# Two mixtures of experts in one pipeline: the second mixture's routing is started one group earlier and spread out

## The chip, the cores and the metric

One core of one Trainium2 chip runs the whole program. The metric is the device time of one execution in microseconds (us). Engines: PE is TensorE (matmul), PEld its weight load, DVE is VectorE, ACT is ScalarE, POOL is GpSimd, SP is SyncE, which only starts DMAs here.

## The reference

The program computes an attention layer, a chunked delta-rule layer and two mixtures of experts, each on x of 8 batches x 512 tokens x 256 channels. The change is in the last part, the two mixtures in a row:

```python
# mixture 0 (cond2): 8 experts of 128, 2 chosen, 256 shared hidden units
logits = (x @ wt.T + g @ wg.T) / 2
scores = softmax(logits); topk_w, topk_idx = top_k(scores, 2); topk_w /= topk_w.sum()
y = sum_k topk_w * (leaky(x @ w_gate[e]) * (x @ w_up[e])) @ w_down[e]   + shared
# mixture 1 (ffn): 16 experts of 64 in 4 groups, 2 groups and then 4 experts chosen, 512 shared units
scores = sigmoid(y @ router_w.T); sb = scores + correction_bias
group_scores = top_k(sb in 4 groups, 2).sum(-1); keep the 2 best groups
topk_idx = top_k(masked sb, 4); w = scores[topk_idx] / sum
out = x + sum_e combine[e] * (silu(y @ gate_w[e]) * (y @ up_w[e])) @ down_w[e]   + shared
```

## The kernel before

`mixtures_phase` works batch by batch. A **group** (m, b) is mixture m on the 512 tokens of batch b. The 16 groups run in the order (0,0), (0,1), (1,0), (0,2), (1,1), ..., (0,7), (1,6), (1,7), so a pair (0,b+1), (1,b) is the steady pattern. A group is cut into **items**, 128 hidden units each: 10 for mixture 0 (items 0 and 1 shared, 8 of one expert each), 12 for mixture 1 (items 0 to 3 shared, 8 of two experts each); 176 items in all. `FIRST[g]` is the first item of group g; q counts items over all groups.

Every engine walks the same list of q, each with an instruction queue of its own, and semaphores order them:

- PE at q: 6 matmuls for the gate (`m_G`) and 6 for up (`m_U`), both L1380 (fp32 as high and low parts), then the side steps of q, then `project_down(q - 2)`, 6 matmuls of the item two back (`m_Y`, L1397). `project_down` waits for `hid_high` and `hid_low` of its item.
- ACT at q: the activation of the gate (L1446; Copy for mixture 0, Silu for mixture 1), its side steps, then the high part of item q-1 (`high`, L1434), then DMA starts of the routing weights (L1480 writes `wT` to DRAM, L1491 reads them back, spread over partitions).
- DVE at q: for mixture 0 the leaky ReLU (L1603), then times up (L1605), for routed items times the routing weights (`weigh`, L1584), its side steps, and at the end the **routing parts** of q (`PARTS[q]`, function `route`).
- POOL at q: the low part of the item (L1523), after ACT's high part.

Side steps (`SIDE[q]`) share one PSUM bank `MB` in the order of the list, each waiting until the one before has been read (`m_bank_free`): `turn` (transpose of x for a batch to come, L1312), `logits` (6 router matmuls, L1329), `rows` (4 small transposes of the logits, L1338, and the exponential on ACT), `weights` (4 transposes of the routing weights, L1347, copied by DVE at L1629 to `wT`), `back` (transposes of the result, L1358, added to x by DVE at L1636). `W_AT[g]` is the item whose side step is `weights` of group g.

The routing parts of mixture 0 are three (`spread`, `choose`, `weigh`), those of mixture 1 are seven: `scores` (ends in a ranking within groups), `groups`, then four rankings `choose0` to `choose3`, one for each 128 tokens (`rank_below`, L997 to L1002, six DVE instructions), and `weigh` (L1572 to L1576). In the kernel before, the logits of (1,b) are computed in item 2 of the mixture 0 group right ahead of it, and the seven parts follow in seven items in a row, 4 to 9 of that group and item 0 of (1,b). The weights of (1,b) are turned at its item 2, the first routed item being item 4. Where a group ends, ACT and DVE take its result out of PSUM in item 1 of the next (`taken_at`).

Of the kernel before, what the change touches and what calls it, by code (L numbers as in the profile page):

```python
# [92 lines left out]
def row(ap, n):  # L93

    return bass.AP(tensor=ap.tensor, offset=ap.offset, ap=[[0, P], [1, n]])
# [909 lines left out]
def mixtures_phase(nc, a, ident, mixture, shared_sems, x1_dram, w_dram, out):  # L1005

    F32R = mybir.dt.float32r
    with ExitStack() as ctx:
# [121 lines left out]
        w_ready = sem("w_ready")  # L1130
# [22 lines left out]
        NG = len(GROUPS)  # L1153
# [8 lines left out]
        SIDE, PARTS, W_AT = {}, {}, {}  # L1162

        def side(q, *steps):
            SIDE.setdefault(q, []).extend(steps)

        def route_from(g, q):

            m = GROUPS[g][0]
            for n, part in enumerate(("spread", "choose", "weigh") if m == 0 else  # L1170
                                     ("scores", "groups", "choose0", "choose1", "choose2", "choose3", "weigh")):
                PARTS.setdefault(q + n, []).append((part, g))
# [5 lines left out]
        PARTS[-1] = [(part, 0) for part in ("spread", "choose", "weigh")]  # L1178
        for g, (m, b) in enumerate(GROUPS):
            q0 = FIRST[g]  # L1180
            W_AT[g] = q0 + (0 if g < 2 else -1 if m == 0 else 2)
            side(W_AT[g], ("weights", g))
            if g == 0:
                side(q0 + N1 - 1, ("turn", 1, 0), ("turn", 1, 1))
                side(q0 + N1 - 1, ("logits", 1), ("rows", 1))
                PARTS[q0 + N1 - 1] = [(part, 1) for part in ("spread", "choose", "weigh")]
            elif m == 0:
                at = 3 if b == 1 else 2
                side(q0 + at, ("logits", g + 1))
                side(q0 + at + 1, ("rows", g + 1))  # L1190
                route_from(g + 1, q0 + at + 2)
                if b >= 2:
                    side(q0 + 4, ("back", b - 2, 0))
                    side(q0 + 5, ("back", b - 2, 1))
            elif b < B - 2:
                side(q0 + 2, ("turn", b + 2, 0))
                side(q0 + 3, ("turn", b + 2, 1))
                side(q0 + 5, ("logits", g + 1))
                side(q0 + 6, ("rows", g + 1))
                route_from(g + 1, q0 + 7)  # L1200
            elif b == B - 2:
                side(q0 + 4, ("logits", g + 1))
                side(q0 + 5, ("rows", g + 1))
                route_from(g + 1, q0 + 6)
            else:
                side(q0 + 4, ("back", b - 1, 0))
                side(q0 + 5, ("back", b - 1, 1))
# [7 lines left out]
        def nth(step):  # L1215

            same = [s for s in FILLS if s[0] == step[0]]
            return same.index(step) + 1
# [5 lines left out]
        def n_shifted(g):  # L1224

            return sum(GROUPS[s[1]][0] == 0 for s in FILLS[:FILLS.index(("rows", g)) + 1] if s[0] == "rows")
# [20 lines left out]
        def routed(q):  # L1247
            g, m, b, i = ITEMS[q]
            return i >= SHARED[m]

        def n_routed(q):

            return sum(routed(j) for j in range(q + 1))
# [19 lines left out]
        with nc.Block() as block:  # L1273
# [149 lines left out]
            @block.scalar  # L1423
            def _(act):
                def high(q):

                    if routed(q):
                        act.wait_ge(weighted, n_routed(q))
                    else:
                        act.wait_ge(mult_up, q + 1)  # L1430
                    if q >= H_SLOTS:

                        act.wait_ge(hid_used, q - H_SLOTS + 1)
                    act.copy(hid_part[0][:, q % H_SLOTS], hid[:, q % G_SLOTS]).then_inc(hid_high, 1)  # L1434

                late = [(lower[:], a["c_lower"]), (cb[:], row(a["L0_ffn_correction_bias"], E2))]
                assert len(late) == N_LATE
                for dst, src in late:
                    act.dma_start(dst, src).then_inc(loaded_late, 16)
                for q in QS:  # L1440
                    if 0 <= q < NQ:
                        act.wait_ge(gate_psum, q + 1)
                        if q >= G_SLOTS:

                            act.wait_ge(hid_low, q - G_SLOTS + 1)
                        act.activation(hid[:, q % G_SLOTS], GB[q % 2][:, :],  # L1446
                                       (ACT.Copy, ACT.Silu)[ITEMS[q][1]]).then_inc(gate_active, 1)
                    for step in SIDE.get(q, ()):
                        if step[0] == "split":
                            m, part, s, (high_w, _, given_w), _, _ = units[step[1]]  # L1450
                            act.wait_ge(w_in[m][part][s], 16 * sum(u[:3] == (m, part, s) for u in units))
                            act.copy(high_w, given_w).then_inc(w_high, 1)
                        elif step[0] == "turn":
                            act.wait_ge(turned, nth(step))
                            act.copy(in0[0][:, step[2]], MB[:, :]).then_inc(in0_high, 1)
                        elif step[0] == "logits":
                            m, b = GROUPS[step[1]]
                            act.wait_ge(logits_psum, nth(step))
                            if m == 0:
                                act.activation(lgT[0:E1, :], MB[0:E1, :], ACT.Identity, scale=0.5,  # L1460
                                               bias=condg[:, b:b + 1]).then_inc(lgT_ready, 1)
                            else:
                                act.copy(lgT[:, :], MB[0:E2, :]).then_inc(lgT_ready, 1)
                        elif step[0] == "rows":
                            m, b = GROUPS[step[1]]
                            if m == 0:
                                act.wait_ge(shifted, n_shifted(step[1]))
                                act.activation(ex[:, :, 0:E1], lg[:], ACT.Exp).then_inc(exps_ready, 1)
                            else:
                                act.wait_ge(rows_psum, nth(step))  # L1470
                                act.activation(ex[:], MB[:, 0:TT * E2].rearrange("p (t e) -> p t e", e=E2), ACT.Exp,
                                               scale=-1.0).then_inc(exps_ready, 1)
                    if 0 <= q - 1 < NQ:
                        high(q - 1)
                    for step in SIDE.get(q, ()):
                        if step[0] == "weights":
                            g = step[1]
                            n = NE[GROUPS[g][0]]
                            act.wait_ge(wT_ready, nth(step))
                            act.dma_start(w_dram[g % 2, 0:n], wT[g % 2][0:n]).then_inc(wT_out, 16)  # L1480
                    for at in W_LOADS.get(q, ()):
                        g, m, b, item = ITEMS[at]
                        slot = (n_routed(at) - 1) % W_SLOTS
                        act.wait_ge(wT_out, 16 * nth(("weights", g)))
                        if n_routed(at) > W_SLOTS:

                            act.wait_ge(weighted, n_routed(at) - W_SLOTS)
                        for e in range(1 + m):
                            part = slice(e * M2, e * M2 + M2) if m else slice(0, P)
                            one = w_dram[g % 2, (1 + m) * (item - SHARED[m]) + e, :]  # L1490
                            act.dma_start(spread[part, slot], bass.AP(tensor=one.tensor, offset=one.offset,  # L1491
                                                                      ap=[[0, part.stop - part.start], [1, L]]))\
                               .then_inc(spread_in[slot], 16)
                    g = taken_at(q)
                    if g is not None:

                        m, b = GROUPS[g]
                        act.wait_ge(hid_used, FIRST[g + 1])
                        if m == 0:
                            for k in range(KD):  # L1500
                                act.copy(in1[b % 2][0][:, k], YB[k][:, :]).then_inc(y_act, 1)
                        else:
                            if b > 0:
                                act.wait_ge(rows_back, 2 * b)
                            act.copy(outT[:, 0], YB[0][:, :]).then_inc(y_act, 1)
# [1084 lines left out]
```

## Time and profile before

| | us |
|---|---|
| median of 3 runs | 2650.97 |
| lowest, highest | 2647.69, 2654.67 |
| the profiled execution | 2649.22 |
| its span in the trace | 2647.4 |
| part of it in the mixtures (first matmul at 1773.1) | 874.3 |
| PE idle in the mixtures waiting for POOL's low part | 24.2, in 25 waits |
| PE idle there waiting for `wT` | 10.2, in 6 waits |

The durations below are those of the profiled execution. Where PE works without a gap, an item shows its first gate matmul 4.2 us after that of the item before it, so the distance between first gate matmuls tells what each item cost.

### The profile page before, as it was taken

How to read it: one execution, taken by the hardware profiler on the slowest of the kernel's cores; microseconds unless marked ns; L12 is line 12 of the kernel's file. 1: busy time of each engine (PE TensorE's matmuls, PEld its weight loads, DVE VectorE, ACT ScalarE, POOL GpSimd, SP SyncE). 2: the span in 40 equal slices, each digit the busy share in tenths (PEclk: the TensorE clock that was granted, in tenths of full speed). 3: DMA queues.
4: the chain of work that ended last, by engine and by line, in shares of the span. 5: the costliest groups of instructions: out<-in, count | busy, mean ns of one | idle time of the engine just before them, and what ended most of it. 6: DMA issues, size and time to landing. Idle time of an engine off the chain costs nothing. (4 is left out here: it accounts for less than half of the span.)

```text
span 2647.4 us, 56555 instructions
## 1 busy us (share of the span) xinstructions
PE 2431.2 (92%) x20838; PEld 2014.3 (76%) x20838; DVE 1711.6 (65%) x4060; ACT 1217.7 (46%) x3095; POOL 1338.6 (51%) x1465
## 2 busy tenths in 40 slices
PE   5999999999999999759999999978899999999998
PEld 3788888888888888537777778856677777777776
DVE  4577677767676767567666766336756747657574
ACT  2666666666666666444544444123333233333332
POOL 3677676767676768166555555215422222322222
PEclk8999999999999999869999999979999999999999
DMA  4000100000000000001122111225021112111211
GB/s 139 7 10 9 44 17 10 10 10 10 10 13 9 7 5 6 13 13 38 46 54 54 41 40 44 64 81 143 23 72 57 49 57 61 61 49 52 64 39 57
DMA packets 156687, 105.03 MB, mean 40 GB/s; under 512 B 85168, under 2 KB 134832, under 8 KB 156416
## 3 DMA queue, kind: packets, MB, share of 16 engines
q1 hardware_dynamic: 131072, 62.83, 8.8%
q10 hardware_dynamic: 25344, 38.60, 4.9%
q8 instruction: 169, 2.77, 0.4%
q14 instruction: 102, 0.84, 0.1%
HBM read 80.51 MB, written 20.88 MB: 38 GB/s over the span
## 5 line engine op out<-in xcount | busy, mean ns | idle before, releaser
L1523 POOL TENSOR_TENSOR m_hid_part<-m_hid,m_hid_part 128x512 fp32r<-128x512 f32 x176 | 239.6, 1361 | 589.6 <-ACT m_hid_part L1434 589.5
L920 POOL TENSOR_TENSOR a_bm<-a_bias,a_mask_add 128x512 f32<-128x512 f32 (+3 forms) x512 | 438.3, 873 | 190.7 <-DVE a_nm L674 186.3
L830 ACT ACTIVATE a_S<-a_S,a_nm 128x512 f32<-128x512 f32 (+3 forms) x512 | 289.3, 565 | 346.7 <-DVE a_nm L674 343.8
L674 DVE CUSTOM_DVE_ANT_0 a_S<-a_S,a_bm,a_nsn 128x512 f32<-128x512 f32 (+3 forms) x512 | 275.6, 545 | 141.5 <-PE a_S L438 137.3
L461 PE MATMUL a_O<-a_v,a_PT 128*128 128x64 f32 x2560 | 342.3, 265 | 0.0
L461 PEld LDWEIGHTS a_O<-a_v,a_PT 128*128 128x128 f32 x2560 | 328.3, 193 | 0.1
L438 PE MATMUL a_S<-a_kT,a_qT 128*128 128x384 f32 (+3 forms) x1024 | 284.2, 359 | 3.5 <-DVE a_nm L674 3.0
L1397 PE MATMUL m_Y<-m_hid_part,m_down_high 128*128 128x512 f32 x704 | 258.6, 408 | 24.9 <-POOL m_hid_part L1523 24.2
L1446 ACT ACTIVATE m_hid<-m_G 128x512 f32<-128x512 f32 x176 | 105.3, 598 | 349.5 <-PE m_G L1380 325.1
L1380 PE MATMUL m_G<-m_in,m_gate_high 128*128 128x512 f32 x704 | 253.0, 400 | 2.5 <-POOL m_up_low L1517 1.6
L1380 PE MATMUL m_U<-m_in,m_up_high 128*128 128x512 f32 x704 | 250.5, 396 | 1.7 <-DVE m_hid L1605 1.7
L448 PE MATMUL a_T<-s_ident,a_S 128*128 128x128 f32 x1280 | 227.0, 275 | 12.3 <-ACT a_PT L839 11.3
L1605 DVE TENSOR_TENSOR m_hid<-m_hid,m_U 128x512 f32<-128x512 f32 x176 | 120.9, 687 | 176.1 <-PE m_U L1380 130.1
L448 PEld LDWEIGHTS a_T<-s_ident,a_S 128*128 128x128 f32 x1280 | 160.3, 140 | 42.3 <-ACT a_S L830 15.7
L1397 PEld LDWEIGHTS m_Y<-m_hid_part,m_down_high 128*128 128x128 f32 x704 | 133.5, 190 | 66.2 <-issue 33.8
L438 PEld LDWEIGHTS a_S<-a_kT,a_qT 128*128 128x128 f32 x1024 | 164.0, 192 | 18.7 <-DVE a_nm L674 6.5
L1434 ACT CAST m_hid_part<-m_hid 128x512 fp32r<-128x512 f32 x176 | 108.4, 616 | 124.6 <-DVE m_hid L1584 103.2
L1380 PEld LDWEIGHTS m_G<-m_in,m_gate_high 128*128 128x128 f32 x704 | 134.0, 190 | 36.0 <-POOL m_up_low L1517 2.1
L1380 PEld LDWEIGHTS m_U<-m_in,m_up_high 128*128 128x128 f32 x704 | 132.6, 188 | 34.8 <-DVE m_hid L1605 2.8
L839 ACT COPY a_PT<-a_T 128x128 f32<-128x128 f32 (+3 forms) x384 | 156.3, 407 | 0.0
L2410 DVE SCALAR_TENSOR_TENSOR d_S<-d_S,d_gm,d_state 128x64 f32<-128x64 f32 x224 | 52.4, 275 | 141.1 <-PE d_state L2139 141.0
L1380 PE MATMUL m_G<-m_in,m_gate_low 128*128 128x512 f32 x352 | 140.7, 400 | 0.0
(314 smaller groups left out, 5392.8 us busy)
## 6 DMA issues: line engine op xcount, KB each, us to landing
m_spread<-s_w ACTq DMA_DIRECT2D x64, 256.0 KB, 3.2
m_spread<-s_w ACTq DMA_DIRECT2D x128, 128.0 KB, 3.0
a_x<-in_x SPq DMA_DIRECT2D x32, 128.0 KB, 2.1
s_hT<-a_hT SPq DMA_DIRECT2D x32, 128.0 KB, 2.1
d_x<-in_x SPq DMA_DIRECT2D x8, 512.0 KB, 4.7
d_h<-s_hT SPq DMA_DIRECT2D x8, 512.0 KB, 4.0
s_xg<-d_xg SPq DMA_DIRECT2D x8, 512.0 KB, 3.0
d_x<-s_xg SPq DMA_DIRECT2D x8, 512.0 KB, 4.6
```

The costliest lines, as they stand in the source:

```text
L438: last = pe.matmul(o_s[:, 0:w], qT[:, tile % 2, h], kT[tile // TT % 2][i][:, 0:w], start=i == 0, stop=i == 1)
L448: last = pe.transpose(TB[n % 2][:, j * P:(j + 1) * P], S[:, n % S_SLOTS, j * P:(j + 1) * P], ident[:])
L461: last = pe.matmul(OB[h // 8][:, (h % 8) * DH:(h % 8 + 1) * DH], PT[:, n % PT_SLOTS, j * P:(j + 1) * P], v[tile // TT % 2][:, j], start=j ...
L674: dve.tensor_tensor_reduce(S[:, n % S_SLOTS, 0:w], SB[n % 2][:, 0:w], bm[:, n % BM_SLOTS, 0:w], -1.0, nsn[:, tile % 2, h:h + 1], ALU.add, ...
L830: act.activation(S[:, n % S_SLOTS, 0:w], S[:, n % S_SLOTS, 0:w], ACT.Exp, scale=-1.0, bias=nm[:, tile % 2, h:h + 1], accum_out=den[:, tile ...
L839: act.copy(PT[:, n % PT_SLOTS, 0:w], TB[n % 2][:, 0:w]).then_inc(s["probsT_act"], 1)
L920: pool.tensor_tensor(bm[:, n % BM_SLOTS, 0:w], bias[:, h, L - w:L], mask_add[b % 2][:, 0:w], ALU.add).then_inc(s["bm_ready"], 1)
L1380: last = pe.matmul(dst[q % 2][:, :], wts[m][j][:, k, item], x[i][:, k], start=(i, j, k) == TERMS[0], stop=(i, j, k) == TERMS[-1])
L1397: last = pe.matmul(YB[k][:, :], down[m][j][:, item, k * P:(k + 1) * P], hid_part[i][:, q % H_SLOTS], start=item == 0 and i + j == 0, stop= ...
L1434: act.copy(hid_part[0][:, q % H_SLOTS], hid[:, q % G_SLOTS]).then_inc(hid_high, 1)
L1523: pool.tensor_tensor(hid_part[1][:, q % H_SLOTS], hid[:, q % G_SLOTS], hid_part[0][:, q % H_SLOTS].bitcast(F32), ALU.subtract).then_inc(hi ...
L1605: dve.tensor_tensor(h, h, UB[q % 2][:, :], ALU.mult).then_inc(mult_up, 1)
```

## The change

Only the order of steps changes; no instruction is added or removed, apart from one wait. For mixture 1 groups (1,0) to (1,5) the list now holds, besides the steps for the mixture 0 group that follows (each moved one item earlier), those of the mixture 1 group after that: its logits in item 8, its rows in item 9, `scores` and `groups` in items 10 and 11, and `choose0` to `choose3` in items 1, 3, 5 and 7 of the mixture 0 group between them, `weigh` in item 8. The weights of groups (1,1) to (1,6) are turned in the last item of the preceding group instead of their own item 2; (1,0) and (1,7) keep item 2. `rows` makes ACT wait until the weights of the group before have been computed, since `ex` and `sc` are single buffers.

```diff
--- before.py
+++ after.py
@@ -1178,26 +1178,30 @@
         PARTS[-1] = [(part, 0) for part in ("spread", "choose", "weigh")]
         for g, (m, b) in enumerate(GROUPS):
             q0 = FIRST[g]
-            W_AT[g] = q0 + (0 if g < 2 else -1 if m == 0 else 2)
+            W_AT[g] = q0 + (0 if g < 2 else 2 if g in (2, NG - 1) else -1)
             side(W_AT[g], ("weights", g))
             if g == 0:
                 side(q0 + N1 - 1, ("turn", 1, 0), ("turn", 1, 1))
                 side(q0 + N1 - 1, ("logits", 1), ("rows", 1))
                 PARTS[q0 + N1 - 1] = [(part, 1) for part in ("spread", "choose", "weigh")]
+            elif m == 0 and b == 1:
+                side(q0 + 3, ("logits", g + 1))
+                side(q0 + 4, ("rows", g + 1))
+                route_from(g + 1, q0 + 5)
             elif m == 0:
-                at = 3 if b == 1 else 2
-                side(q0 + at, ("logits", g + 1))
-                side(q0 + at + 1, ("rows", g + 1))
-                route_from(g + 1, q0 + at + 2)
-                if b >= 2:
-                    side(q0 + 4, ("back", b - 2, 0))
-                    side(q0 + 5, ("back", b - 2, 1))
+                side(q0 + 4, ("back", b - 2, 0))
+                side(q0 + 5, ("back", b - 2, 1))
             elif b < B - 2:
                 side(q0 + 2, ("turn", b + 2, 0))
                 side(q0 + 3, ("turn", b + 2, 1))
-                side(q0 + 5, ("logits", g + 1))
-                side(q0 + 6, ("rows", g + 1))
-                route_from(g + 1, q0 + 7)
+                side(q0 + 4, ("logits", g + 1))
+                side(q0 + 5, ("rows", g + 1))
+                route_from(g + 1, q0 + 6)
+                side(q0 + 8, ("logits", g + 2))
+                side(q0 + 9, ("rows", g + 2))
+                for n, part in ((10, "scores"), (11, "groups"), (13, "choose0"), (15, "choose1"), (17, "choose2"),
+                                (19, "choose3"), (20, "weigh")):
+                    PARTS.setdefault(q0 + n, []).append((part, g + 2))
             elif b == B - 2:
                 side(q0 + 4, ("logits", g + 1))
                 side(q0 + 5, ("rows", g + 1))
@@ -1463,6 +1467,8 @@
                                 act.copy(lgT[:, :], MB[0:E2, :]).then_inc(lgT_ready, 1)
                         elif step[0] == "rows":
                             m, b = GROUPS[step[1]]
+                            if step[1] > 0:
+                                act.wait_ge(w_ready, step[1])
                             if m == 0:
                                 act.wait_ge(shifted, n_shifted(step[1]))
                                 act.activation(ex[:, :, 0:E1], lg[:], ACT.Exp).then_inc(exps_ready, 1)
```

## Rows read from the trace of the kernel before

**Rows 1.** The page's busy time of each engine, its share of the span, instructions.

```profile
PE 2431.2 (92%) x20838; PEld 2014.3 (76%) x20838; DVE 1711.6 (65%) x4060; ACT 1217.7 (46%) x3095; POOL 1338.6 (51%) x1465
```

**Rows 2.** Idle time of PE by what ended it, 1990 to 2560 us (total, times, longest).

```profile
PE m_Y L1397 <- POOL m_hid_part L1523: 16.7, 18, 1.0
PE m_M L1312 <- DVE m_wT L1629: 9.3, 5, 1.9
PE m_Y L1397 <- DVE m_in L1644: 0.7, 1, 0.7
```

**Rows 3.** PE in order of time (start us, us, line, operation); first gate matmul of items.

```profile
2207.81 0.40 PE L1380 MATMUL m_G<-m_in,m_gate_high 128*128 128x512 f32 x1
...
2213.16 0.39 PE L1380 MATMUL m_G<-m_in,m_gate_high 128*128 128x512 f32 x1
...
2218.54 0.40 PE L1380 MATMUL m_G<-m_in,m_gate_high 128*128 128x512 f32 x1
...
2223.93 0.40 PE L1380 MATMUL m_G<-m_in,m_gate_high 128*128 128x512 f32 x1
...
2229.21 0.63 PE L1312 MATMUL m_M<-s_ident,m_x_turn 128*128 128x128 f32 x4 [1.87 <-DVE m_wT L1629]
...
2231.07 0.40 PE L1380 MATMUL m_G<-m_in,m_gate_high 128*128 128x512 f32 x1
...
2235.71 0.40 PE L1380 MATMUL m_G<-m_in,m_gate_high 128*128 128x512 f32 x1
...
2254.48 0.40 PE L1380 MATMUL m_G<-m_in,m_gate_high 128*128 128x512 f32 x1
...
2267.10 0.40 PE L1380 MATMUL m_G<-m_in,m_gate_high 128*128 128x512 f32 x1
...
2271.73 0.39 PE L1380 MATMUL m_G<-m_in,m_gate_high 128*128 128x512 f32 x1
```

**Rows 4.** Busy time of each engine in two equal stretches: PE, PEld, DVE, ACT, POOL, clock.

```profile
2095.00:2200.00 105.00, 100.34 (x437) 79.20 (x436) 65.32 (x118) 34.27 (x57) 29.44 (x22) 0.98 0.18 53
2200.00:2305.00 105.00, 100.33 (x444) 79.29 (x443) 66.75 (x124) 34.40 (x57) 29.44 (x22) 1.00 0.19 57
```

**Rows 5.** DVE in order of time, items 4 to 8 of group (0,4).

```profile
2191.05 0.18 DVE L1554 TENSOR_SCALAR m_ex<-m_ex 128x64 f32<-128x64 f32 x1
...
2196.34 0.69 DVE L1605 TENSOR_TENSOR m_hid<-m_hid,m_U 128x512 f32<-128x512 f32 x1
...
2198.27 0.21 DVE L1559 TENSOR_TENSOR m_rest<-m_sbias,m_sel 128x64 f32<-128x64 f32 x1
...
2202.46 0.69 DVE L1605 TENSOR_TENSOR m_hid<-m_hid,m_U 128x512 f32<-128x512 f32 x1
...
2207.88 0.69 DVE L1605 TENSOR_TENSOR m_hid<-m_hid,m_U 128x512 f32<-128x512 f32 x1
...
2210.45 1.38 DVE L1000 TENSOR_TENSOR m_gt<-m_gt,m_ge 128x256 f32<-128x256 f32 x1
```

**Rows 6.** POOL in order of time, around the last row of rows 5.

```profile
2210.02 1.53 POOL L1523 TENSOR_TENSOR m_hid_part<-m_hid,m_hid_part 128x512 fp32r<-128x512 f32 x1 [3.86 <-ACT m_hid_part L1434]
```

**Rows 7.** DVE in order of time, a ranking of group (0,5) computed during group (1,3).

```profile
2257.58 0.69 DVE L1605 TENSOR_TENSOR m_hid<-m_hid,m_U 128x512 f32<-128x512 f32 x1 [1.02 <-PE m_U L1380]
...
2259.04 0.41 DVE L997 TENSOR_TENSOR m_gt<-m_sc 128x256 f32<-128x256 f32 x1
...
2261.19 0.18 DVE L1002 TENSOR_SCALAR m_sel<-m_sel 128x32 f32<-128x32 f32 x1
```

**Rows 8.** DVE in order of time, routing weights of group (1,3).

```profile
2223.89 0.22 DVE L1572 TENSOR_TENSOR m_w<-m_sc,m_sel 128x64 f32<-128x64 f32 x1
...
2224.81 1.27 DVE L1576 TENSOR_TENSOR m_w<-m_w,m_wsum 128x64 f32<-128x64 f32 x1
```

**Rows 9.** PE in order of time, items 2 and 4 of group (1,2).

```profile
2117.81 0.40 PE L1380 MATMUL m_G<-m_in,m_gate_high 128*128 128x512 f32 x1
...
2131.13 0.40 PE L1380 MATMUL m_G<-m_in,m_gate_high 128*128 128x512 f32 x1
```

## The prediction

> **What bounds the kernel now.** I read the page's busy times first: PE is busy 92% of the span [rows 1], so a change of order can win only what PE stands still. Next the waits of PE in the mixtures, from 1990 to 2560 us, the part that the change reorders: 18 waits for POOL's low part (16.7 us), 5 for `wT` (9.3 us) and one for DVE's subtraction of `m_in` (0.7 us) [rows 2], and nothing else. Then PE in order of time, for where these waits are [rows 3]. An item without side steps takes (2267.10 - 2254.48) / 3 = 4.21 us. In the group (1,3) and the item before it, the distances are 5.35 (item 9 of (0,4)), 5.38 (item 0), 5.39 (item 1), 7.14 (item 2), 4.64 (item 3, one `turn`). So there are three slow items, and a fourth in which `weights` and `turn` meet in the one bank: PE stands 1.87 us until DVE has copied `wT`.
>
> Last, why POOL is late. DVE's times, beside its due time, tell it. A multiplication by up is due 3.1 us after the item's first gate matmul (2254.48 to 2257.58, [rows 3, 7]). Item 7 of (0,4) started two undisturbed items before 2207.81, at 2199.4, so it was due at 2202.5; DVE did it at 2207.88 [rows 5], 5.4 late. Item 6 was due at 2198.3 and done at 2202.46, 4.2 late, and cost PE nothing; the lag of 5.4 cost 1.14 in item 9. So PE bears a lag of about 4.3 us, its two items of distance less the high and low parts. Once there, each further item with a ranking costs as much as DVE needs for it: 5.42 us from 2202.46 to 2207.88, against 4.21. DVE is the bound for some 30 us of each pair of groups, and PE for the rest: in 105 us DVE is busy only 66.8 [rows 4]. It has room, but not where its work is bunched.
>
> **The change, part by part.**
>
> Moved rankings. Taken away from DVE in six consecutive mixture 0 items and one more: `scores` with the next leaky ReLU 5.3 us (2191.05 to 2196.34), so `scores` 4.6; `groups` with it 4.2 (2198.27 to 2202.46), so 3.5; each `choose` 5.42 less multiplication and weighting (1.46, rows 7's first two) and leaky ReLU (0.7), so 3.3 [rows 5, 7]. The sum is unchanged, the place is new. In the old place `choose` is stretched: its L1000 took 1.38 us while POOL's low part ran from 2210.02 to 2211.55 [rows 5, 6]. A ranking of the same 256 elements per partition that met no POOL work took 2.35 from first start to last end (2259.04 to 2261.37) [rows 7].
>
> Is the new place too full? I carry the lag of DVE on from item 10 of (1,b), where it comes in on time:
> - item 10: 1.5 + `scores` 4.6 = 6.1 against 4.2; lag 1.9.
> - item 11: 1.5 + copy of `wT`, 0.6, + `groups` 3.5, + leaky ReLU 0.7 = 6.3 against 4.6 (one `weights`); lag 3.6 at item 0 of mixture 0.
> - item 0, shared: 1.4 against 4.2; lag 0.8.
> - item 1: multiplication, copy of the result, `choose0` at its dear price, leaky ReLU: 0.7 + 0.7 + 3.3 + 0.7 = 5.4; lag 2.0.
> - item 2: 2.2; back on time. Items 3, 5, 7 with a `choose`: 4.6 to 5.5, or 5.2 to 6.1 in item 5 with its `back`, against 4.2 and 4.6; lags of 0.4 to 1.5, each gone in the next item.
> The largest, 3.6, stays under the 4.3 that PE bears, and falls on an item without weighting, which helps the low part. So I price the new rankings at nothing; PE's matmuls cover them. With the margin of 0.7 gone, each microsecond over would cost PE one in each of the 6 pairs, 6 us in all.
>
> Whether a `choose` costs 2.35 or 3.3 there: the Trainium skill ("SBUF — State Buffer", the section "SBUF: two separate sides") has VectorE and GpSimd hold a shared port pair exclusively, so an instruction with two SBUF inputs waits for the whole of POOL's. That agrees with L1000 ending just after POOL's end. By the rule an early `choose` in a routed item is over before POOL begins and costs 2.35; by the dear row it costs 3.3. The saving is the same by both, since either lag is under 4.3.
>
> Gain of it: item 9 of six groups (0,2) to (0,7), 6 x 1.14 = 6.8 us; items 0 and 1 of (1,1) to (1,6), 6 x (1.17 + 1.18) = 14.1 us [rows 3].
>
> Moved weights. The transposes cost 4.63 - 4.21 = 0.42 (2267.10 to 2271.73, an item with `weights`), `turn` 0.43 (4.64 - 4.21). Item 2 loses 7.14 - 4.21 - 0.42 - 0.43 = 2.08 us; the 0.42 is paid in item 9 instead, where no step of the bank follows until the `turn` two items later. Five groups: 10.4 us [rows 2, 3]. In (1,6), which has no `turn`, the wait of 0.7 for `m_in` goes [rows 2]. Now `w` has to be there a whole item earlier: `weigh` runs in item 8, on PE's side due 4.2 us after item 8's due time. Lag 0.4 to 1.3, multiplication and weighting 1.5, five small instructions 1.1 (2223.89 to 2224.81, and 0.2 for the last undisturbed) or 2.2 with the last one held to 1.27 [rows 7, 8]: 3.0 to 5.0. I take 3.0 to 3.9, nothing lost; at the far end 0.8 in each of 6 groups, 5 us. Behind that wait on PE stand `project_down` and the next item.
>
> DMAs. The write of `wT` and the reads for items 4 to 6 of mixture 1 no longer start together in item 3 but one item's worth at a time from item 1, on ACT's queue. ACT's activation was not the bound there before; no gain, no loss. SP's and POOL's queues are passed by nothing.
>
> Steps moved from mixture 0 item 2 and 3 to mixture 1 items 8 and 9 (`logits`, `rows`) cost PE the same there. The exponential now comes an item after mixture 0's; Exp and Silu alternate as often. The new wait of ACT for `w_ready` stands in `rows`: ahead of it nothing is open, because `weigh` of the group ahead (item 8) ends some 3 us after its item's due time and PE's `rows` comes 4.2 after. Behind it on ACT is the high part of item 8 and the activation of item 10. Cost nothing; if `weigh` were a microsecond later than PE's transposes, those two are late by it, which the 4.3 still bears.
>
> TensorE's clock. After the 1.87 us stand in (1,2) items 2 and 3 took 13.32 us (2117.81 to 2131.13) against 11.78 in (1,3) (2223.93 to 2235.71): 1.5 us more, and the stretch around it shows a mean granted clock of 0.98 of full speed against 1.00 [rows 3, 4, 9]; of the two levels, 1.2 and 2.4 GHz, some matmuls had the lower. Without the stand I count 1.5 gained. The Trainium skill ("TensorE: Matmul & The Clock Gate", the section on HAM oscillation) asks for longer idle gaps than this before the clock falls; by it the sum would be 1.5 less, 32.0. The trace disagrees, as the fall follows the gap directly.
>
> **Sum.** 6.8 + 14.1 + 10.4 + 0.7 + 1.5 = 33.5 us. The profiled execution took 2649.22, its span 2647.4, so it becomes 2615.7. It lies 1.75 below the median of the runs, 2650.97, from which 33.5 gives 2617.5. I predict 2617.
>
> **The rivals.**
> - Stalls shrink but stay: the burst of items 10 and 11 exceeds 4.3. For: the margin is only 0.7, and the weighting is held by POOL at times. Against: the lag peaks on one item. Price 0.5 to 2 us in each of 6 groups: 2620 to 2630. Chance 0.11.
> - `w` comes late, as worked out, and the whole of item 9's gain goes as well: 5 + 6.8 to both: 2629 to 2640. Chance 0.04.
> - Nothing moves: DVE is the bound over the whole pair, so that waits only change place. Then 2651. Against: DVE 66.8 of 105 us. Chance 0.02.
> - Slower: ACT's wait for `w_ready` in item 9. If `weigh` of the group ahead came late, the activation of item 10 and so `gate_psum`'s release would hold PE. PE loses only what exceeds the tolerance; `weigh` has 1.2 us in hand, PE's tolerance is 4.3, and to pass 2659 the six pairs must lose 33.5 + 8.5 = 42 us, 7 each: so it decides only where `weigh` is 12.5 us later than the rows let it be, and then gives 2660. Chance 0.02.
> - The forecast, all stalls gone: 2617, own range 2611 to 2622. Chance 0.81.
>
> **How the numbers follow.** The range 2610 to 2630 takes in the forecast and the first rival; the runs' own spread, 3.3 below the median and 3.7 above, is within it. What a measurement of this kernel can tell from no change is about 0.3%, 8 us. Faster by more: 0.81 + 0.11 + 0.04 less a little, 0.95. Within: 0.03, the case in which nothing moves and the edge of the one above it. Slower: 0.02.
>
> **What would show it.** In the profile after: PE's waits for POOL's low part down from 25 to about 7 (those of the start and the end), the waits for `wT` down from 6 to 1; distances of 4.2 in items 0 and 1 and 4.64 in items 2 and 3 of mixture 1, 4.63 in item 9 of mixture 0; L1000 shorter in the mean; a pair of groups in 99.0 us instead of 104.6 (2117.81 to 2223.93 less the clock's 1.5, [rows 3, 9]), as 1.14 + 1.17 + 1.18 + 2.08 go. Wrong would be: waits of PE for POOL two items after items 10 and 11, at the `weights` step for `w` (L1576), or a DVE lag that does not clear in the items without a ranking.

## The result

The changed kernel took 2625.39 us (median of 4 runs, 2622.33 to 2627.34) against 2649.94 for the kernel before in the same comparison: ratio 0.9904, 95% interval 0.9887 to 0.9921, so 24.6 us faster. Forecast were 2617 (range 2610 to 2630) and a gain of 33.5 us. The profiled execution took 2626.46, span 2624.7.

Forecast and measured time differ by 8 us, and the time misses the forecast's own range of 2611 to 2622. The page's busy line after it, as [rows 1] before:

```profile
PE 2429.4 (93%) x20838; PEld 2017.6 (77%) x20838; DVE 1695.6 (65%) x4060; ACT 1215.2 (46%) x3095; POOL 1337.0 (51%) x1465
```

PE's work is what it was; only standing time went. DVE's busy time fell by 16.0 us (1711.6 to 1695.6) with the same 4060 instructions. PE's waits from 1773 to 2625 us, the whole of the mixtures (before: 24.2 us in 25 waits for POOL and 10.2 in 6 for `wT`), by what ended them; total, times, longest. The wait in the steady part alone (1964 to 2560) follows:

```profile
PE m_Y L1401 <- POOL m_hid_part L1529: 11.1, 12, 1.4
PE m_M L1351 <- DVE m_w L1582: 7.4, 3, 3.4
...
PE m_M L1316 <- DVE m_wT L1635: 0.9, 1, 0.9
```

```profile
PE m_Y L1401 <- POOL m_hid_part L1529: 3.6, 5, 0.7
```

The 18 waits for POOL and 5 for `wT` of [rows 2] are gone, but 5 new ones of 0.72 us stand in their place, and a sixth in (1,0). PE in order of time shows where, for the group (1,3), first gate matmuls of items 0, 2, 4, 6 and 7 (as [rows 3]):

```profile
2207.59 0.39 PE L1384 MATMUL m_G<-m_in,m_gate_high 128*128 128x512 f32 x1
...
2215.99 0.40 PE L1384 MATMUL m_G<-m_in,m_gate_high 128*128 128x512 f32 x1
...
2225.27 0.40 PE L1384 MATMUL m_G<-m_in,m_gate_high 128*128 128x512 f32 x1
...
2235.61 0.40 PE L1384 MATMUL m_G<-m_in,m_gate_high 128*128 128x512 f32 x1
...
2239.31 0.47 PE L1401 MATMUL m_Y<-m_hid_part,m_down_high 128*128 128x512 f32 x1 [0.72 <-POOL m_hid_part L1529]
...
2240.77 0.40 PE L1384 MATMUL m_G<-m_in,m_gate_high 128*128 128x512 f32 x1
```

Items 0 and 1 are 4.20 us each, items 2 and 3, with a `turn` each, 4.64, items 4 and 5 with logits and rows 10.34 in sum. Item 6 has no side step and takes 5.16: PE stands 0.72 us ahead of the down projection of item 4, for POOL.

The clean measure of the change is the stretch from the first gate matmul of (0,2) to that of (1,6): 1956.46 to 2526.88 before, 570.42 us, and 1964.34 to 2507.42 after, 543.08. A second profile of the changed kernel gave 543.06. The part ahead of the mixtures, which no edit here touches, ended anywhere from 1774.9 to 1790.6 in twelve profiled executions (first gate matmul of the mixtures), and from there to (0,2) it was 173.6 to 179.2 us more. So the total of one execution hides effects of a few microseconds, and the stretch doesn't.

**Why item 6.** ACT in order of time, item 5 of (1,3) after the change:

```profile
2232.48 0.60 ACT L1450 ACTIVATE m_hid<-m_G 128x512 f32<-128x512 f32 x1 [1.61 <-PE m_G L1384]
2235.77 1.28 ACT L1474 ACT_TABLE_LOAD   x1 [2.69 <-DVE m_lg L1630]
...
2237.06 0.23 ACT L1474 ACTIVATE m_ex<-m_lg 128x32 f32<-128x32 f32 x1
2237.20 0.60 ACT L1438 CAST m_hid_part<-m_hid 128x512 fp32r<-128x512 f32 x1
```

and the same step in the kernel before (its item 6):

```profile
2247.76 1.28 ACT L1468 ACT_TABLE_LOAD   x1
2250.38 0.23 ACT L1468 ACTIVATE m_ex<-m_lg 128x32 f32<-128x32 f32 x1 [1.34 <-DVE m_lg L1624]
2250.52 0.60 ACT L1434 CAST m_hid_part<-m_hid 128x512 fp32r<-128x512 f32 x1
```

### The profile page after: what moved, and what is told of

Same layout as the page of the kernel before. It is cut to its first block and busy times, and to the rows that moved or that the text cites. A ratio compares the mean times of both kernels' runs of the same rounds, so it can differ in the third digit from the quotient of the medians.

```text
span 2624.7 us, 56570 instructions
## 1 busy us (share of the span) xinstructions
PE 2429.4 (93%) x20838; PEld 2017.6 (77%) x20838; DVE 1695.6 (65%) x4060; ACT 1215.2 (46%) x3095; POOL 1337.0 (51%) x1465
## 5 line engine op out<-in xcount | busy, mean ns | idle before, releaser
L1401 PE MATMUL m_Y<-m_hid_part,m_down_low 128*128 128x512 f32 x352 | 139.8, 397 | 0.0
```

The source lines that it names most:

```text
L1401: last = pe.matmul(YB[k][:, :], down[m][j][:, item, k * P:(k + 1) * P], hid_part[i][:, q % H_SLOTS], start=item == 0 and i + j == 0, stop= ...
```

## The experiments

The ratios are to the kernel before, each with its own runs of it on the same chip. Its median there was 2652.58 us for e1 to e4, 2656.32 for e5 to e8 and 2647.67 for e9 and e10, so medians of different comparisons can't be set side by side to a few microseconds; "the stretch" is that from (0,2) to (1,6), of the profiled execution.

**e1: the two waits in the other order** (the edit shortened).

```diff
-if step[1] > 0: act.wait_ge(w_ready, step[1])
 if m == 0:
     act.wait_ge(shifted, n_shifted(step[1]))
+    if step[1] > 0: act.wait_ge(w_ready, step[1])
     ...
 else:
     act.wait_ge(rows_psum, nth(step))
+    act.wait_ge(w_ready, step[1])
```

> The changed kernel with the two waits ahead of each exponential in the other order (first for its input, then for the routing weights); nothing else. Theory: the activation table load takes over the first-named of two waits when there are two, so in the changed kernel it stands behind its input (2.7 us idle before it in item 5 of mixture 1), ends 1.28 us later and makes the high and low parts of item 4 late, 0.95 us in item 6 of each of six groups. Swapped, the load stands behind the wait that has long been met: items 6 back to 4.2 us, no wait of PE for POOL there, 5 to 6 us off the changed kernel's 2625, so about 2619.5. Rival: the 0.95 us comes from logits and rows having moved one item ahead, next to the first routed items and their DMAs; then nothing changes, 2625.

Measured: 2613.13 us (2610.19 to 2619.23), ratio 0.9852 (0.9826 to 0.9879). ACT in item 5 of (1,3), then PE's first gate matmuls of items 6 and 7:

```profile
2225.34 1.28 ACT L1474 ACT_TABLE_LOAD   x1
2227.97 0.23 ACT L1474 ACTIVATE m_ex<-m_lg 128x32 f32<-128x32 f32 x1 [1.35 <-DVE m_lg L1631]
```

```profile
2227.86 0.40 PE L1384 MATMUL m_G<-m_in,m_gate_high 128*128 128x512 f32 x1
...
2232.07 0.40 PE L1384 MATMUL m_G<-m_in,m_gate_high 128*128 128x512 f32 x1
```

(The expectation calls the wait that the load takes over the first-named; in the program it is the one written last, here that for `w_ready`, long met.) The load is back ahead of the input's wait, item 6 takes 4.21, and PE doesn't stand at all in the steady part. The stretch is 538.32 us, 4.8 less than the changed kernel's, five times 0.95. The theory holds; the median lies 12 us under the first of the changed kernel, more than item 6 can give (see e9 and e10).

**e2: the kernel before with only the new wait.**

```diff
 elif step[0] == "rows":
     m, b = GROUPS[step[1]]
+    if step[1] > 0:
+        act.wait_ge(w_ready, step[1])
```

> The kernel before with only the changed kernel's wait for the routing weights ahead of each exponential; order of steps as before. Theory of the table load: the exponential for mixture 0, computed in item 6 of mixture 1 groups, has its load 1.28 us later, of which the trace of before has some 0.6 us in hand, so item 7 grows by about 0.7 to 0.9 us in six or seven groups: 4 to 6 us slower than before, about 2655. Rival, the moved steps are to blame: no change, 2650.

Measured: 2657.66 us (2647.9 to 2667.78), ratio 1.0018 (0.9999 to 1.0037). ACT, and PE where it stands:

```profile
2247.24 1.28 ACT L1470 ACT_TABLE_LOAD   x1 [2.69 <-DVE m_lg L1626]
```

```profile
2250.77 0.47 PE L1397 MATMUL m_Y<-m_hid_part,m_down_high 128*128 128x512 f32 x1 [0.72 <-POOL m_hid_part L1525]
```

The order of steps is that of before, and the same late load and the same 0.72 us appear, in item 7 (5.17 instead of 4.21). The interval of the ratio reaches 1, but the slow item is there in all of the groups (1,0) to (1,5). So the wait alone brings it, without the moved logits and rows. The stretch is 573.73, 3.3 more than before. Five slow items are 4.8; the 1.5 of the clock's fall, which this execution had no part of, makes the difference.

**e6: the wait ahead of mixture 1's exponential alone.** DVE computes the routing weights of the group ahead earlier than mixture 0's `m_lg`, in its own order, so the one wait implies the other.

```diff
-if step[1] > 0:
+if m == 1:
     act.wait_ge(w_ready, step[1])
```

> The changed kernel with its new wait only ahead of mixture 1's exponential; ahead of mixture 0's it is left out, where the wait for its input already implies it (DVE computes both in order). Theory of the table load: mixture 0's load goes ahead of the wait again, item 6 is back to 4.2 us, the same time as with the swapped waits, 2613 to 2619, though mixture 1's load still stands behind its input: that one is covered. Rival: both loads have to be freed; then about half of the gain, 2620.

Measured: 2624.46 us (2621.03 to 2625.4), ratio 0.9876 (0.9838 to 0.9914). ACT:

```profile
2234.17 1.28 ACT L1474 ACT_TABLE_LOAD   x1
2236.80 0.23 ACT L1474 ACTIVATE m_ex<-m_lg 128x32 f32<-128x32 f32 x1 [1.35 <-DVE m_lg L1630]
```

The load is free again and the stretch is 538.33, that of e1. The median is nearly that of the first comparison of the changed kernel and misses the forecast of 2613 to 2619. The profiled execution took 9.2 us more than e1's, and 8.8 of that lie ahead of the stretch: the first gate matmul of (0,2) came at 1967.3 against 1958.5. By the items the theory holds; by the total nothing can be told.

**e3: the routing weights of mixture 1 turned in its item 2 again.**

```diff
-W_AT[g] = q0 + (0 if g < 2 else 2 if g in (2, NG - 1) else -1)
+W_AT[g] = q0 + (0 if g < 2 else 2 if m == 1 else -1)
```

> The changed kernel, but the routing weights of mixture 1 turned in its own item 2, as before; the early and spread rankings stay. It measures what of the gain is the moved weights alone. If the wait of turn for the copy of the weights is the bank's own round trip it stays at about 0.9 us in each of five groups: 4 to 5 us slower than the changed kernel, 2630. If the 1.87 us of before were all due to the bunched bank steps and not to the late DVE, they stay whole: 9 to 10 us slower, 2635. If the early rankings alone had removed it: no change, 2625.

Measured: 2630.01 us (2619.54 to 2640.74), ratio 0.9919 (0.9889 to 0.9948). PE in item 2 of (1,3), between its own and the next first gate matmul:

```profile
2208.03 0.40 PE L1384 MATMUL m_G<-m_in,m_gate_high 128*128 128x512 f32 x1
...
2212.53 0.63 PE L1316 MATMUL m_M<-s_ident,m_x_turn 128*128 128x128 f32 x4 [1.09 <-DVE m_wT L1635]
...
2214.39 0.40 PE L1384 MATMUL m_G<-m_in,m_gate_high 128*128 128x512 f32 x1
```

Item 2 takes 6.36, that is 1.30 more than its matmuls and transposes (4.21 + 0.43 + 0.42). The stretch is 549.20, 6.1 more than the changed kernel's. So of the 2.08 us of before, 1.30 is the bank's own round trip from one step to the next (transposes, DVE's copy, the next transpose) and 0.78 was the late DVE: its copy began 0.27 us after the end of the transposes here (2211.44 to 2211.71) and 1.05 before (2227.34 to 2228.39). The expected 0.9 was too little.

**e4: begun as early, but the seven parts in a row.**

```diff
-for n, part in ((10, "scores"), (11, "groups"), (13, "choose0"), (15, "choose1"), (17, "choose2"),
-                (19, "choose3"), (20, "weigh")):
-    PARTS.setdefault(q0 + n, []).append((part, g + 2))
+route_from(g + 2, q0 + 10)
```

> The changed kernel, begun as early, but the seven routing parts in seven items in a row (items 10, 11 of mixture 1 and items 0 to 4 of mixture 0) instead of the four rankings in every second item. Theory: the lag of DVE is carried from item to item; it is near 4 us after item 12, passes the 4.3 us that PE bears in items 13 to 15 and costs about 1.1 us in each of two or three items of six pairs: 14 to 20 us slower than the changed kernel, 2640 to 2645. Rival: an early start alone is enough, as nothing waits for the weights; no change, 2625.

Measured: 2671.51 us (2668.13 to 2676.53), ratio 1.0071 (1.0045 to 1.0097): slower than before, and over twice what I expected it to lose. PE in (0,4), items 2 and 5, and DVE just ahead of both waits:

```profile
2192.46 0.40 PE L1382 MATMUL m_G<-m_in,m_gate_high 128*128 128x512 f32 x1
...
2196.94 0.47 PE L1399 MATMUL m_Y<-m_hid_part,m_down_high 128*128 128x512 f32 x1 [1.51 <-ACT m_hid_part L1436]
...
2198.41 0.40 PE L1382 MATMUL m_G<-m_in,m_gate_high 128*128 128x512 f32 x1
...
2207.26 0.40 PE L1382 MATMUL m_G<-m_in,m_gate_high 128*128 128x512 f32 x1
...
2213.86 1.08 PE L1360 MATMUL m_M<-s_ident,m_outT 128*128 128x128 f32 x4 [3.62 <-DVE m_res L1640]
...
2217.30 0.63 PE L1382 MATMUL m_G<-m_in,m_gate_high 128*128 128x512 f32 x1
```

```profile
2195.50 0.69 DVE L1609 TENSOR_TENSOR m_hid<-m_hid,m_U 128x512 f32<-128x512 f32 x1
...
2196.11 0.68 DVE L1654 COPY m_outT<-m_Y 128x512 f32<-128x512 f32 x1
...
2211.70 0.69 DVE L1609 TENSOR_TENSOR m_hid<-m_hid,m_U 128x512 f32<-128x512 f32 x1
...
2213.03 0.68 DVE L1640 TENSOR_TENSOR m_res<-m_M,m_res 128x512 f32<-128x512 f32 x1
```

Item 2 is 5.95 us. The profile puts its wait of 1.51 down to ACT's high part, but this is the projection of item 0, whose low part was done at 2193.79. As the first of its group it waits also until the result of the group before is out of PSUM, and DVE's copy of that (L1654) ended at 2196.79. Item 5 is 10.0: PE stands 3.62 us ahead of the second `back`, until DVE has read the first one out of the bank (L1640 at 2213.03), and the matmuls after it take 0.63 us instead of 0.40, at a granted clock of 0.50 from 2213.9 to 2219.2, the lower of the two levels, 1.2 GHz.

Neither is a wait for the low part, which the theory looked for. It had reckoned only with the down projection of an item two back, which bears a lag of 4.3 us. DVE's multiplication of item 1 came 4.2 late (2195.50, due at 2191.3) and cost 1.5; that of item 4 came 6.0 late (2211.70, due at 2205.7) and cost 3.6. So, as an estimate from these rows, taking out the result bears 2.7 us and a step of the shared bank 2.4.

**e5: e4 with `back` in items 7 and 8.**

```diff
-side(q0 + 4, ("back", b - 2, 0))
-side(q0 + 5, ("back", b - 2, 1))
+side(q0 + 7, ("back", b - 2, 0))
+side(q0 + 8, ("back", b - 2, 1))
```

> The early bunched version, with the two back steps of the mixture 0 groups in items 7 and 8 instead of 4 and 5. Theory: of its item 5 of 10.0 us, some 5.4 us are the second back waiting for DVE to read the first out of the shared bank, because a late DVE is felt by a bank step after one item and by the down projection only after two. Moved to where DVE has caught up, that wait goes, and what is left are waits for the low part in items 2, 5 and 6, together 3 to 4 us in each of six pairs: about 2647, 22 us slower than the changed kernel. Rival: the bunched rankings themselves cost all of it and the wait only moves to another place; then it stays near 2671.

Measured: 2639.34 us (2632.12 to 2648.3), ratio 0.9942 (0.992 to 0.9965). PE's waits in the mixtures:

```profile
PE m_Y L1399 <- POOL m_hid_part L1527: 17.2, 24, 1.4
PE m_Y L1399 <- ACT m_hid_part L1436: 9.1, 6, 1.5
```

Of the 7 waits for `m_res` in e4's mixtures (22.6 us) one of 0.9 at the end is left. Items 2, 5 and 6 of the mixture 0 groups take 5.95, 4.8 and 5.13: 3.2 us a pair over the spread version (103.14 against 99.95), as expected, but only items 5 and 6 (1.5 us) by waits for the low part. The 1.7 of item 2 is again the wait for the result to be taken out: these are the six waits of 9.1 us that the view gives to ACT. The stretch is 562.31, against 588.30 in e4 and 543.08 in the changed kernel: 19.2 more, 6 x 3.2, where the median shows 14. A pair of groups, (1,3) with (0,5), takes 107.01 in e4, 103.14 in e5, 99.95 in the changed kernel, 104.58 before.

**e7 and e8: the routing of (1,0), which no edit had spread, begun one item earlier in (0,1);** in e8 also with a gap in item 7 and the last ranking and the weights together in item 0 of (1,0). Both with e1's swapped waits; the two edits in one, shortened:

```diff
-side(q0 + 3, ("logits", g + 1)); side(q0 + 4, ("rows", g + 1)); route_from(g + 1, q0 + 5)
+side(q0 + 2, ("logits", g + 1)); side(q0 + 3, ("rows", g + 1))
+route_from(g + 1, q0 + 4)                       # e7
+for n, part in ((4, "scores"), (5, "groups"), (6, "choose0"), (8, "choose1"), (9, "choose2"),
+                (10, "choose3"), (10, "weigh")): # e8, in place of route_from
+    PARTS.setdefault(q0 + n, []).append((part, g + 1))
```

> The swapped waits, and the routing of (1,0), the one that is still bunched, begun one item earlier in (0,1). It ends one item earlier, so the 3.4 us that PE waits for its weights in item 2 of (1,0) goes, and the low clock after it; the waits for the low part stay: 4 to 5 us faster than the swapped kernel's 2613, 2609. Rival: the seven parts are bound by DVE, and the wait moves ahead one item: 2613.

> The same, with a gap in item 7 of (0,1), the last ranking in item 0 of (1,0) and the weights in the same item. By the theory of the lag the gap takes one or two of the waits for the low part away as well (1.0 to 1.4 us each), the end of the routing staying ahead of item 2: 6 to 8 us faster than the swapped kernel, 2606. Rival: item 0 with ranking and weights makes the weights late again: like the swapped kernel, 2613.

Measured: e7 2619.05 us (2611.72 to 2621.03), ratio 0.9851 (0.9821 to 0.9882); e8 2624.4 (2618.18 to 2625.12), ratio 0.9872 (0.9842 to 0.9901). Both medians miss their forecasts, and neither ratio is clearly under e1's 0.9852. In e7 item 2 of (1,0) fell from 10.99 us to 7.14, but items 7 to 9 of (0,1) grew by 2.0 in sum, and `turn` waits for `wT`:

```profile
PE m_M L1351 <- DVE m_w L1583: 3.5, 2, 2.9
...
PE m_M L1316 <- DVE m_wT L1636: 1.9, 1, 1.9
```

So half of it only moves ahead, where the rival had all of it do so; some 2 us of the two groups are left, which the medians don't resolve. In e8 item 2 is 11.05, as in e1: the weights are late again, as its rival had it.

**e9 and e10: the changed kernel and e1 once more, on one chip in the same rounds.** No edit.

> The changed kernel once more, on the same chip and in the same rounds as the swapped one, since the time ahead of the mixtures, which no edit touches, differed by up to 16 us between profiled executions. Theory: 0.957 us in item 6 of six mixture 1 groups, as in its first profile; total 2625 where before is 2650, whatever the chip's offset.

> The kernel with the swapped waits once more beside it. Theory: item 6 at 4.2 us, the rest of the mixtures item by item the same, so 5.7 us less than the changed kernel run beside it, give or take the clock's falls in the parts ahead; the 12 us between the two medians so far were half chance. Rival: the swap gives the whole 12 us, through something outside item 6 that the item distances would then show.

Measured: 2620.57 us (2616.36 to 2622.81), ratio 0.9894 (0.9869 to 0.9919), and 2615.84 (2607.09 to 2625.34), ratio 0.9879 (0.9852 to 0.9906). First gate matmuls of (0,2) and of (1,6), in e9 and in e10:

```profile
1958.62 0.39 PE L1384 MATMUL m_G<-m_in,m_gate_high 128*128 128x512 f32 x1
```

```profile
2501.68 0.39 PE L1384 MATMUL m_G<-m_in,m_gate_high 128*128 128x512 f32 x1
```

```profile
1962.04 0.39 PE L1384 MATMUL m_G<-m_in,m_gate_high 128*128 128x512 f32 x1
```

```profile
2500.37 0.39 PE L1384 MATMUL m_G<-m_in,m_gate_high 128*128 128x512 f32 x1
```

543.06 and 538.33: 4.7 us, the same as the difference of the medians here, though their intervals overlap. Item 6 of (1,0) and 0.4 us in (1,7), which also goes with the swap, add to it: about 6 us. So of the 12 us between the first medians about half are not the swap's.

## Why the prediction was right, and which step was off

**The bound and the room.** Right. DVE was late only where its work was bunched; it has the same instructions after the change and PE's standing time went. e4 shows it from the other side: the same work, bunched, in the new place costs more than before.

**The lag of DVE, item by item.** Right to some tenths. DVE in order of time after the change: the multiplications of item 11 of (1,2) and of items 0 to 3 of (0,4), whose first gate matmuls stand at 2159.6, 2164.2, 2168.4, 2172.6 and 2176.8, and the first and last row of `choose1`:

```profile
2164.75 0.69 DVE L1611 TENSOR_TENSOR m_hid<-m_hid,m_U 128x512 f32<-128x512 f32 x1
...
2170.99 0.69 DVE L1611 TENSOR_TENSOR m_hid<-m_hid,m_U 128x512 f32<-128x512 f32 x1
...
2172.31 0.69 DVE L1611 TENSOR_TENSOR m_hid<-m_hid,m_U 128x512 f32<-128x512 f32 x1
...
2177.50 0.69 DVE L1611 TENSOR_TENSOR m_hid<-m_hid,m_U 128x512 f32<-128x512 f32 x1
...
2179.91 0.69 DVE L1611 TENSOR_TENSOR m_hid<-m_hid,m_U 128x512 f32<-128x512 f32 x1
...
2181.41 0.41 DVE L997 TENSOR_TENSOR m_gt<-m_sbias 128x256 f32<-128x256 f32 x1
...
2183.57 0.17 DVE L1002 TENSOR_SCALAR m_sel<-m_sel 128x16 f32<-128x16 f32 x1
```

Due 3.1 us after those, the multiplications come 2.1, 3.7, 0.8, 1.8 and 0.0 late; forecast were 1.9, 3.6, 0.8, 2.0 and 0. The largest stays under the 4.3 that PE bears, and PE doesn't stand. The prediction held every lag against that one limit; e4 shows two followers that bear only 2.4 to 2.7. Here the lags ahead of them are 0.8 (item 1) and 0.4 (item 4), so the omission cost nothing; that was luck, since the prediction had not asked. A `choose` in a routed item takes 2.33 (2181.41 to 2183.74), the cheap one of the two prices; `choose0` in item 1 takes 3.2, the dear one. L1000 fell in the mean from 1133 ns to 585 (1990 to 2560 us).

**Gain of the moved rankings.** Item 9 of mixture 0 is 4.21 + 0.42 for the weights, items 0 and 1 of mixture 1 4.2, as forecast: 6.8 and 14.1 us.

**Gain of the moved weights.** Right in sum: 2.08 in item 2, and `w` was there in time (its last instruction ended at 2204.9, PE's transposes in item 9 of (0,4) came at 2205.8). e3 adds how it divides, 1.30 and 0.78, which the prediction did not.

**The clock.** No profiled execution of the changed kernel or of e1 shows a fall in the steady part, and e2, with all the old waits, had none either in the stretch. So the five gaps of 1.87 us brought one fall in one execution and none in the other. The 1.5 us were right for the profiled execution of before; for its other executions no trace shows them.

**The new wait of ACT: the step that was off.** "Cost nothing", the prediction said, since `w_ready` is long met and a lateness is borne. The first is true and beside the point: the wait cost PE through the table load that now stands behind the input's wait. The term priced at 0 measured 0.95 us in six groups, 5.7 us, and went with the order of two lines (e1), with the wait left out (e6), and came with the wait alone (e2). I had noted that Exp and Silu alternate as often as before and not asked when the loads run; the trace of before shows the load (2247.76) ahead of the wait that ends in the activation (2250.38). They do alternate as often: 28 loads in the mixtures, before and after. (They don't stand "an item" apart, as the prediction has it, but in items 5 and 9.)

**The sum.** In the stretch 27.3 us were gained (570.42 to 543.08). The forecast for it is 6.8 + 5 x 2.35 + 5 x 2.08 + 1.5, and 1.93 for logits and rows of (1,1), which moved out of it, less 0.42 for the weights of (1,6), which moved in: 32.0. The 4.8 between are five of the new waits. The rest of the distance from 33.5 to the 24.6 of the medians is the sixth, 0.4 us in (1,7), and some 2.8 us that lie within the runs' own spread.

**The signs.** Of what it said would show it, PE waited for POOL's low part 12 times and not 7, six of them the new ones, and for `wT` once, as forecast; a pair took 99.95 us and not 99.0. Of the signs of being wrong none came in the steady part. The wait that did come, in item 6, was not among them.

**The rivals.** The first, lesser stalls of 0.5 to 2 us a group for 2620 to 2630, gives the right size and time, but by another mechanism: not a burst of DVE in items 10 and 11, but ACT in item 5. That the measured time lies in the range of 2610 to 2630 is therefore in part luck: the range was widened for a rival that did not come. The late `w`, DVE as the bound of the pair and ACT held by `w_ready` itself were all not there. (The second rival's 2629 is 2617 and 11.8; its far end, 2640, has no working.)

**The best version.** e1 took 0.9852 and 0.9879 of before in two comparisons, with 98.99 us a pair, which is the forecast's 99.0. e7, at 0.9851, is some 2 us shorter by its items; no run tells the two apart by time. Busy times of e10 from 1970 to 2490 us: PE has no gap left and the clock stays at 1.00.

```profile
1970.00:2490.00 520.00, 520.00 (x2313) 416.44 (x2312) 336.73 (x647) 178.34 (x298) 155.97 (x116) 1.00 0.20 61
```

## What to carry to other kernels

An engine that isn't the bound over a stretch can still be it over five items; carry its lag from item to item, against what each follower bears, and give each follower its own limit: here a projection two items behind bore 4.3 us, a step that waits for a shared bank or for a result to be taken out only 2.4 to 2.7. Where the profile names what ended a wait, check that it is something that this instruction waits for in the program: in e4 it named a cast of another item.
## What the runs showed of the hardware that I had not expected

**The untouched part varies most.** The first gate matmul of the mixtures stood at 1774.9 us in e2 and at 1790.6 in e8, with the same code ahead. Busy times from 1250 to 1765 us, with the granted clock (PE, PEld, DVE, ACT, POOL, clock), first in e2, then in e8:

```profile
1250.00:1765.00 515.00, 495.23 (x8610) 390.83 (x8608) 308.53 (x690) 202.62 (x433) 238.03 (x345) 0.96 0.19 47
```

```profile
1250.00:1765.00 515.00, 505.70 (x8624) 399.30 (x8618) 308.61 (x691) 201.76 (x431) 241.15 (x347) 0.93 0.19 46
```

The clock was 0.96 in one and 0.93 in the other, PE busy 495 against 506 us; why it differs, no run shows. The opening of the mixtures varies too: item 0 of (0,1) took 7.47 us in one profiled execution of the changed kernel and 11.14 in the other. In the mixtures' steady part, with the clock at 1.00, five executions of four programs with the same order in it (e1, e6, e7, e8, e10) agree within 0.01 us over 538 us.

**VectorE instructions of a few elements wait for POOL too.** In (0,4), DVE and POOL after the change:

```profile
2168.55 1.15 DVE L1569 TENSOR_SCALAR m_goff<-m_gsel 128x16 f32<-128x16 f32 x1
```

```profile
2168.36 1.31 POOL L1529 TENSOR_TENSOR m_hid_part<-m_hid,m_hid_part 128x512 fp32r<-128x512 f32 x1 [4.61 <-ACT m_hid_part L1438]
```

A multiply-add with one tensor input of 16 elements a partition took 1.15 us and ended just after POOL's low part (2168.36 to 2169.67). It took 1.15 in all six groups where the change moved it, and 0.17 to 0.18 in the other two and in all eight before; so it isn't only instructions with two tensor inputs that are held. The Trainium skill ("SBUF — State Buffer", section "Who interferes with whom") has `tensor_scalar` contend with GpSimd where it can use two ports. The trace agrees that this one contends; whether it used two ports, no run shows.
